# Score pass of a graph layer: rows of destinations and kinds are broadcast as bytes and widened by ScalarE into single buffers before the comparisons

## The reference, cut to what matters

```
xn = layernorm(x)                          # 6250 nodes x 256
Q, K, V = enh @ Wq + bq, ...               # 4 heads of 64
mod_k  = K[src] + 0.2 * rel_w[kind][:, None, :]        # 100000 edges, 64 kinds
scores = einsum('ehd,ehd->eh', Q[dst], mod_k) / 8
w      = softmax of scores over the edges of one dst
agg    = segment_sum(w * V[src], dst)
x = x + layernorm(agg @ Wo + bo + xn) * gamma + beta + mix(xn)
x = x + ffn(layernorm(x))                  # 8 experts, one per token
```

## Time and profile before

| | us |
|---|---|
| median of 3 runs | 2440.83 |
| lowest, highest | 2439.93, 2443.38 |
| the profiled execution | 2438.15 |
| its span | 2436.4 |
| score pass, first gather issued to last reduction's end | 195.6 to 1265.8 |

### The profile page before, as it was taken

The page is one execution under the profiler, slowest core; times in us unless marked ns, Lnnn a source line. Parts: engine busy times, 40 slices in busy tenths (PEclk is TensorE's granted clock), DMA queues, the critical chain, the costliest instruction groups (busy, mean ns, idle before and its releaser), DMA issues. The chain is left out here.

```text
span 2436.4 us, 50363 instructions
## 1 busy us (share of the span) xinstructions
PE 1969.0 (81%) x11356; PEld 1408.1 (58%) x11357; DVE 1799.0 (74%) x3100; ACT 869.7 (36%) x2796; POOL 1456.7 (60%) x1360
## 2 busy tenths in 40 slices
PE   8965777776777777777757999999889999679996
PEld 4533444554554544444545777777655555468885
DVE  6877999999999999999967888878776764321111
ACT  4532111111111111111116777777445555432221
POOL 4655777777777777777732777777654542023442
PEclk9987888888888888888878999999899999889998
DMA  6658999999999999999996888888534643464450
GB/s 218 222 177 275 359 362 358 361 360 354 360 362 355 363 356 359 358 358 360 349 231 205 304 277 278 280 278 277 170 130 169 219 159 119 172 232 168 154 186 36
DMA packets 388111, 649.78 MB, mean 267 GB/s; under 512 B 40235, under 2 KB 235951, under 8 KB 387925
## 3 DMA queue, kind: packets, MB, share of 16 engines
q1 hardware_dynamic: 200132, 277.43, 34.7%
q0 software_dynamic: 77824, 262.55, 30.2%
q10 hardware_dynamic: 110096, 109.07, 12.8%
HBM read 471.00 MB, written 178.83 MB: 267 GB/s over the span
## 5 line engine op out<-in xcount | busy, mean ns | idle before, releaser
L721 POOL DMA_INDIRECT s_kv<-kv_d,s_index x832 | 791.3, 951 | 266.0 <-issue 238.0
L1362 PE MATMUL a_sum_ps<-a_w,a_is_dst 128*128 128x260 f32 x1760 | 403.6, 388 | 20.5 <-DVE sums L1333 11.9
L1275 POOL TENSOR_TENSOR a_w<-a_v,a_w 128x512 f32<-128x512 f32 x220 | 299.1, 1365 | 164.8 <-ACT a_w L1232 107.5
L1362 PEld LDWEIGHTS a_sum_ps<-a_w,a_is_dst 128*128 128x128 f32 x1760 | 328.2, 191 | 95.8 <-issue 25.1
L867 PE MATMUL s_q_ps<-q,s_is_dst 128*128 x2496 | 366.9, 304 | 10.0 <-DVE s_key L776 8.7
L820 PE MATMUL s_mv_ps<-s_mixed 128*128 128x128 f32 x416 | 106.4, 436 | 272.2 <-DVE s_mixed L756 272.2
L771 DVE TENSOR_TENSOR s_key<-s_kv,s_rel_ps 128x1024 f32<-128x1024 f32 x208 | 253.3, 1218 | 63.0 <-issue 36.4
L867 PEld LDWEIGHTS s_q_ps<-q,s_is_dst 128*128 128x128 bf16 x2496 | 253.3, 107 | 79.2 <-issue 12.7
L1248 ACT ACTIVATE a_w<-a_v,a_w 128x64 f32<-128x64 f32 x1100 | 285.8, 335 | 3.5 <-DMA a_v<-v_d 3.5
L1309 DVE SCALAR_TENSOR_TENSOR a_is_dst<-node_of,first_node,a_col_ps 128x256 f32<-128x256 f32 x440 | 208.8, 475 | 82.7 <-PE a_sum_ps L1362 64.9
L781 DVE TENSOR_REDUCE s_part<-s_key 128x16 f32<-128x1024 f32 x208 | 253.7, 1220 | 10.7
(11 more groups left out here) (310 smaller groups left out, 2941.4 us busy)
## 6 DMA issues: line engine op xcount, KB each, us to landing
a_v<-v_d SPq DMA_DIRECT2D x440, 256.0 KB, 3.7
v_d<-s_kv ACTq DMA_DIRECT2D x208, 512.0 KB
s_local<-local_d SPq DMA_DIRECT2D x106, 256.0 KB, 6.0
xh_d<-h_hid SPq DMA_DIRECT2D x24, 1024.0 KB, 7.5
s_kind<-type_d SPq DMA_DIRECT2D x212, 64.0 KB, 6.6
s_kv<-kv_d,s_index POOLq DMA_INDIRECT x832
kv_d<-pkv SPq DMA_DIRECT2D x50, 256.0 KB, 2.0
wd<-in_L_ffn_Wd SPq DMA_DIRECT2D x8, 1024.0 KB, 12.0
```

Of the source, the lines that this page charges most:

```text
L721: nc.gpsimd.indirect_dma_start(out=kv[:, g * GROUP + b, :], out_offset=None, in_=R["kv"], in_offset=bass.IndirectOffsetOnAxis(ap=index[:, ...
L1275: nc.gpsimd.tensor_tensor(heads(w[:, at, mine, 0:C]), heads(v[:, g, mine, :]), w[:, at, mine, C:, None].broadcast_to([P, len(tiles), H, D] ...
L1362: ins = nc.tensor.matmul(sum_ps[(g * PAIRS + k) % BANKS][:], is_dst[:, g % WRING, 2 * k + u, :], w[:, g % WRING, 2 * k + u, :], start=(u = ...
```

## The change

Destinations and kinds are kept as bytes in the tile stage and in HBM. In the tile stage the conversion of `local` moves from ACT to GpSimd and cuts values at 255; the host gives the 128 edges behind the last the destination 6656 and the kind 64 in place of -1 (their source stays -1), so that they match no lane. In the score pass SP broadcasts into byte buffers with two slots, ACT's new function `widen` casts a half into bf16 buffers `local` and `kind` with one slot each, and DVE compares from these. `widen` waits for the row loads and for the comparison before it; DVE waits for `widen` by two semaphores, and SP's next loads too.

```diff
-        local_b = sb("t_local_b", [TS_ROWS, TS_COLS * P], BF16)
-        type_b = sb("t_type_b", [TS_ROWS, TS_COLS * P], BF16)
+        local_b = sb("t_local_b", [TS_ROWS, TS_COLS * P], U8)
+        type_b = sb("t_type_b", [TS_ROWS, TS_COLS * P], U8)
...
+            pool.wait_ge(S["local_set"], 1)
+            nc.gpsimd.tensor_scalar(by_tile(local_b), local[:], 255.0, None, ALU.min).then_inc(S["local_stored"], 1)
...
-            act.wait_ge(S["local_set"], 1)
-            nc.scalar.copy(by_tile(local_b), local[:]).then_inc(S["local_stored"], 1)
...
-        local = sb("s_local", [P, 2, HALF * P], BF16)
-        kind = sb("s_kind", [P, 2, GROUP * P], BF16)
+        local_in = sb("s_local_in", [P, 2, HALF * P], U8)
+        kind_in = sb("s_kind_in", [P, 2, GROUP * P], U8)
+        local = sb("s_local", [P, HALF * P], BF16)
+        kind = sb("s_kind", [P, GROUP * P], BF16)
...
-                    sp.wait_ge(S["onehot_ready"], i * (RING // 2) + h + 1)
+                    sp.wait_ge(S["local_wide"], i * (RING // 2) + h + 1)
+                    sp.wait_ge(S["kind_wide"], i * (RING // 2) + h + 1)
...
+            def widen(h, n, loads):
+                act.wait_ge(rows_in[h], loads * 48)
+                act.wait_ge(S["onehot_ready"], n)
+                act.nop(nofuse=True)
+                nc.scalar.copy(local[:], local_in[:, h, :]).then_inc(S["local_wide"], 1)
+                nc.scalar.copy(kind[:], kind_in[:, h, :]).then_inc(S["kind_wide"], 1)
...
                     store(at[0], i, more)
+                    widen(0, i * (RING // 2) + 2 * b + 2, i * RINGS + b + 2)
                     squares(n)
...
                     store(at[2], i, more)
+                    if more or b == 0:
+                        widen(1, i * (RING // 2) + 2 * b + 3, i * RINGS + b + 2)
                     store(at[3], i, more)
...
+            for h in range(2):
+                widen(h, h, 1)
...
-                dve.wait_ge(rows_in[h], n)
-                nc.vector.tensor_scalar(is_dst[:, h, :], local[:, h, :], M["lane"][:], None, ALU.is_equal)\
+                dve.wait_ge(S["local_wide"], n)
+                nc.vector.tensor_scalar(is_dst[:, h, :], local[:], M["lane"][:], None, ALU.is_equal)\
                   .then_inc(S["steps"], 1)
-                nc.vector.tensor_scalar(is_kind[:, h, :], kind[:, h, :], M["lane64"][:], None, ALU.is_equal)\
+                dve.wait_ge(S["kind_wide"], n)
+                nc.vector.tensor_scalar(is_kind[:, h, :], kind[:], M["lane64"][:], None, ALU.is_equal)\
                   .then_inc(S["onehot_ready"], 1)
...
-         "local": dram("local_d", (TS_ROWS + 2, TS_COLS * P), BF16), "type": dram("type_d", (TS_ROWS + 2, TS_COLS * P), BF16),
+         "local": dram("local_d", (TS_ROWS + 2, TS_COLS * P), U8), "type": dram("type_d", (TS_ROWS + 2, TS_COLS * P), U8),
...
+    arrays["edges"][E:, 1:] = NPAD, NREL
```

More of the change, by code:

```diff
@@ L10 @@
 I32 = mybir.dt.int32
+U8 = mybir.dt.uint8
 ALU = mybir.AluOpType
@@ L601, in stage_scores @@
                  "mk_done mv_done sq_ready mvs_ready ss_ready rr_ready vkv_ready skv_ready rkv_ready mks_ready "
-                 "dots_done dots_added dots_zeroed")
+                 "dots_done dots_added dots_zeroed local_wide kind_wide")
         S = {n: sem("s_" + n) for n in names.split()}
@@ L610, in rows_of @@
             def rows_of(h, n):
-                sp.dma_start(local[:, h, :], row(R["local"], n)).then_inc(rows_in[h], 16)
+                sp.dma_start(local_in[:, h, :], row(R["local"], n)).then_inc(rows_in[h], 16)
                 for k in range(2):
-                    sp.dma_start(kind[k * NREL:(k + 1) * NREL, h, :],
+                    sp.dma_start(kind_in[k * NREL:(k + 1) * NREL, h, :],
                                  R["type"][bass.ds(n, 1), k * GROUP * P:(k + 1) * GROUP * P]
@@ L793, in _ @@
             dve.wait_ge(S["qr_free"], 2)
-            onehots(0, 48)
+            onehots(0, 1)
             with dve.Fori(0, RTURNS) as i:
@@ L799, in _ @@
                     if g % 2 == 0:
-                        onehots((h + 1) % 2, (i * RINGS + (h + 1) // 2 + 1) * 48)
+                        onehots((h + 1) % 2, i * (RING // 2) + h + 2)
                     n = i * 2 + g // 4 + 1
```

## The result

The changed kernel takes 2446.33 us (median of 15 runs, 2441.93 to 2450.73) against 2441.04 for the kernel before in the same comparison (15 runs, 2439.09 to 2443.38): a ratio of 1.0021 with an interval of 1.0014 to 1.0027. That is 5.3 us slower, just beyond the 0.2% (4.9 us) that I had set as "no change", and outside my range, which ended at 2445.0. The profiled execution took 2445.7 us with a span of 2444.0 (before 2438.15 and 2436.4). So the two traces differ by 7.6 us, more than the medians do: the execution profiled before was faster than each of the 15 runs of that kernel here, of which the fastest took 2439.09.

The account below looks back on a forecast made before the run. The prediction took GpSimd's gathers to pace the score pass, with the DMA engines bounding its last 46 us. +0.6 (tile stage) - 2.0 (row loads) + 0 = -1.4 us gave 2439.4 us, range 2433 to 2445.

Parts of the forecast that it names:

- GpSimd's gathers: Score pass: the 832 gathers keep their duration and gap; priced 0, or -4 us if less traffic removes their excess.
- Rival C: Score pass: the widening ahead of the squares makes VectorE the bound; 17 us slower, 2458; chance 5%.
- the 2% for a slowdown: Whole kernel: chance of 2% for an unseen slowdown, as smaller scratch rows in HBM move the tensors behind them.
- GpSimd paces, VectorE and the DMA engines don't.: Score pass: GpSimd sets the pace with a gather every 1.256 us, though VectorE and the DMA engines look full.
- Row loads, -2.0 in the tail: Score pass: halved row bytes save 2.0 us in the DMA-bound last 46 us, bounds -2.8 and 0; nothing earlier.
- my price per MB: End of the score pass: SP's queue time per MB loaded, 3.3 us over the pass or 4.8 in the tail.
- The casts, 1.05 + 0.60 us, price 0: Score pass, ScalarE: a widening pair takes 1.65 us, bounds 1.1 and 2.4, covered by VectorE's idle time, so 0.
- The room: Score pass, block head: squares end 1.55 us before VectorE's norms; with 1.32 us idle, a pair costs from 2.87 us.
- Comparisons and second wait, 0: Score pass, VectorE: comparisons stay at 0.505 and 0.379 us, and the added second wait costs 0.
- The excess of the gathers over their median, -4 or 0: Score pass: gathers' 951 ns mean over 946 median, 4 us in all; -4 if less traffic removes it, 0 taken.
- rival A: Score pass: the DMA engines bound the whole pass, so halved row bytes save 56 us, time 2385; chance 4%.
- The tile stage, +0.6: Tile stage: GpSimd's new operation, 1.2 us, at most 2.3, delays VectorE's `t_valid`; +0.6 us, bounds 0 and +2.3.

Follow-up runs that it names:

- e1: The changed kernel with the conversion of the destinations to bytes back on ScalarE: 2442.45 us against 2444.82 for the kernel before, ratio 0.9994.
- e2: The kernel before plus GpSimd's minimum with 255 in the tile stage, into a tile nobody reads: 2451.9 us against 2444.82, ratio 1.003.
- e6: e2 with the GpSimd minimum writing bf16 in place of bytes: 2450.41 us in one execution, beside 2445.16 of the kernel before.
- e3b: e3 run again on another chip, where the kernel before took 2439.83: 2455.02 us, ratio 1.0057.
- e10: The changed kernel with a small GpSimd copy behind its minimum: 2710.42 us, beside 2708.66 of the kernel before on a slower chip.
- e3: The kernel before with byte rows that VectorE compares itself, without casts: 2712.47 us, beside 2708.66 of the kernel before on a slower chip.
- e11: e1 with the 1024-column cast made three times in each widening: 2708.8 us, beside 2708.66 of the kernel before on a slower chip.
- e5: The kernel before with the absent edges' sources spread over 128 nodes in place of one row: 2425.73 us against 2444.82, ratio 0.9918.
- e11b: e11 run again on another chip, where the kernel before took 2439.83: 2479.28 us, ratio 1.0158.
- e7: e2 with a plain GpSimd copy from f32 to bytes in place of the minimum: 2445.88 us in one execution, beside 2445.16 of the kernel before.
- e8: e2 with a small GpSimd copy behind the minimum: 2447.67 us in one execution, beside 2445.16 of the kernel before.
- e10b: e10 run again on another chip, where the kernel before took 2439.83: 2441.8 us, ratio 1.0003.

## Why the prediction was wrong

The step that failed is "GpSimd's gathers", priced at 0 with bounds of -4 and 0. I asked only whether less traffic would make a gather shorter, and set no bound above, although I had put a new kind of operation on the engine that paces the pass: the change's only way to cost something 832 times over. Measured: 7 ns in the minimum and median, 10 in the mean, +8.0 us from first to last gather. Rival C, my case for slower, named another mechanism; the 2% for a slowdown "that I don't see" held what came, but not for the reason given there (moved tensors), since e1 moves them too and has the old gathers.

Point by point:

- **GpSimd paces, VectorE and the DMA engines don't.** Right. e1 halves the bytes for nothing, and where the gathers' durations change (the change, e2, e6, e3b) the time follows them. Where another thing sets the pace (e10, e3, e11) it doesn't.
- **Row loads, -2.0 in the tail.** Not seen; it would be too small to resolve. SP's queue took 0.67 MB and 6.3% of 1225 to 1262 us, before 0.92 and 11.9%, so the DMA work did go; but from the last gather to VectorE's last group it is 22.5 us for 22.8, the groups stay 7.75 us apart (1224.14 to 1270.67, six of them), and e1's ratio of 0.9994 has 1 in its interval. That the DMA engines bound the tail was right, but what filled them was one row read again and again (e5), which my price per MB knew nothing of.
- **The casts, 1.05 + 0.60 us, price 0.** Right: 1045 and 613 ns. The room was used up nearly to its end, as the timelines of ScalarE and, behind it, VectorE show in the block of the earlier trace rows:

```profile
611.57 1.04 ACT L676 CAST s_local<-s_local_in 128x1024 bf16<-128x1024 uint8 x1
612.52 0.61 ACT L677 CAST s_kind<-s_kind_in 128x512 bf16<-128x512 uint8 x1
613.04 0.59 ACT L688 ACTIVATE s_mixed<-s_mk_ps 128x512 f32<-128x512 f32 x1
613.53 0.59 ACT L690 ACTIVATE s_mixed<-s_mv_ps 128x512 f32<-128x512 f32 x1
```

```profile
614.19 1.21 DVE L760 TENSOR_REDUCE s_ss<-s_mixed 128x16 f32<-128x1024 f32 x1
```

  The squares end at 614.12, 0.07 us ahead of the norms; before, 1.55. Over the 42 blocks from 300 to 1150 us it is 0.03 to 0.67 us, before 1.10 to 1.90. e11b shows that there is a point from which it costs, about where the sum had it.
- **Comparisons and second wait, 0.** Right: 512 and 369 ns, idle before them 0.0.
- **The excess of the gathers over their median, -4 or 0.** 0 was right, the reason wrong. The excess is not DMA traffic but the comparisons: in the trace of before all 4.3 us of it lie in the 59 gathers that start inside one. Such a gather takes 1.02 us (GpSimd)

```profile
607.59 1.02 POOL L721 DMA_INDIRECT s_kv<-kv_d,s_index  x1 [0.30 <-issue]
```

  beside this comparison (VectorE),

```profile
607.45 0.33 DVE L732 TENSOR_SCALAR s_is_kind<-s_kind,lane 128x512 bf16<-128x512 bf16 x1
```

  and e3b makes it grow with the comparisons' length, to 21 us. In the trace of the change it is 6.4 us, which are the 2 us beyond 832 x 7 ns; why more gathers meet a comparison there (72 for 59) no run separates. The traffic, rival A's bound, had no part in the pace: with 359 GB/s before and 340 in e1 it is 1043.6 and 1043.7 us from the first gather to the last.
- **The tile stage, +0.6.** Right in size and mechanism (+0.72 on `t_valid`), but the operation's 3.80 us lay above my bound of 2.3, taken from a copy and a two-input operation. That the operation was longer costs nothing here.

What stays open: what inside GpSimd lasts from the minimum until the copy. That the last operation decides is shown by e2, e6, e7, e8 and e10b; the mechanism isn't in any trace, and whether another operation with a constant than the minimum does the same was not run. The gathers of the tile stage ahead of the operation (median 987 ns), and those of a later stage, which index fills and a select precede (933/942), have their old durations, which fits.

## What to carry to other kernels

When an engine paces a stage by many equal short instructions, ask of every edit what it does to the duration of one of them, also an edit that comes long before on that engine; compare minimum and median, not busy share, since 10 ns in the mean of a gather are 8 us here, and 7 of them showed in the shortest. Give each term a bound on both sides, above all the one that is multiplied by the largest count. Fewer bytes are worth nothing while the queue's feeder paces; look instead at what the padding reads, which was worth 19 us.

## What the runs showed of the hardware

- A GpSimd minimum with a constant (3.80 us for 104x1024 from f32, a copy to bytes 2.09) leaves all 832 indirect gathers of the next stage 7 ns longer at the minimum (949 for 942, median 953 or 957 for 946) over 1050 us; a GpSimd copy of 0.28 us between them takes that away (e8, e10b).
- A VectorE comparison holds a gather that starts inside it: 1.02 us beside a bf16 comparison of 0.33 us, 1.28 beside byte comparisons of 0.74 and 0.48; in the mean 1.02 (59 gathers, before) and 1.18 (70, e3b) for 0.946. The f32 operations of 1.22 us beside nearly all other gathers don't.
- While the gathers all read one row, all traffic is 204 GB/s with DMA engines that look full (1.01); with the reads spread over 128 rows, 301 GB/s at 0.87.
- ScalarE widens bytes to bf16 at about the rate of its copies from f32: 1045 ns for 1024 columns (1.06 us), 613 for 512.
